# Cross-attention on one core: fp16 pairs in place of fp32r pairs, all sixteen heads in one pass

## Chip, core and metric

The kernel runs on one core of one Trainium2 chip. The metric is the device time of the whole program in microseconds. Its engines are TensorE (PE in the profile; its weight loads are PEld), VectorE (DVE), ScalarE (ACT), GpSimd (POOL) and SyncE (SP), which here only issues DMAs.

## What is computed

Sixteen batches; 512 query rows, 512 context rows and width 512 in each; 16 heads of 64.

```python
Q = (x @ Wq + bq); K = (ctx @ Wk + bk); V = (ctx @ Wv + bv)      # 512 x 1024, split into 16 heads
scores = einsum('bhqd,bhkd->bhqk', Q, K) / 8 * mask
attn = softmax(scores, axis=-1)
out = einsum('bhqk,bhkd->bhqd', attn, V).reshape(b, s, 1024) @ Wo + bo
x = x + out
return (x - mean(x)) * rsqrt(var(x) + 1e-5) * gamma + beta
```

All inputs and outputs are float32. To keep near float32 precision, the kernel writes each operand of a matmul as a pair, a rounded value (hi) and the difference that the rounding left (lo), and adds three products for each: hi·hi, hi·lo and lo·hi.

## The kernel before, in words

Work is done in tiles of 128 partitions by 512 columns. Two heads make a *pair* (128 wide). The sixteen heads are cut into two groups of eight (`GROUPS = 2`, four pairs in a group); the program goes through all sixteen batches with the weights of group 0, then again through all sixteen with the weights of group 1, so there are 32 *half-batches*. After group 0 the sum x + bo + part of the output is stored to a DRAM buffer `partial`, and group 1 reads it back, adds its part and does the layer norm.

In each half-batch TensorE does:

- 16 *fills* (`fill`, lines 340 to 342): Q0 to Q3 and K0 to K3 (one pair of heads each), V0 to V3 (128 rows of the context each) and O0 to O3 (128 rows of the output each). Each is 4 contraction tiles times 3 products, 12 matmuls of 128x128 weights and 512 columns. The operands are fp32r.
- 16 *score queries* (`scores`, lines 388 to 394): for a pair and 128 query rows, two heads side by side in the two row halves of the array, 3 products: 3 steps of two matmuls each, fp32r.
- 4 *values* (`values`, line 423): for one pair, 12 steps of two matmuls in the two column halves of the array. The operands (probabilities and V) are already fp16 pairs.
- one 1-column matmul (L404), `bound_inputs`, for a bound on V from which its fp16 scale is made.

For each tile of 128x512 scores: DVE multiplies by the mask and takes the row maximum (`mask_and_max`, L709), POOL negates two maxima (`negate_max`, L976), ACT takes the exponential with its row sum (`exponentials`, L526), POOL scales four sums (L983), DVE inverts them (L718), ACT rounds the normalized tile to fp16 (`round_probs`, L539), DVE takes the fp16 difference (`split_probs`, L725), for one tile in eight POOL does instead, in two instructions (L991, L996). Then a DMA transpose on SP's queue brings the two heads' pieces of 128 query rows into `pT`. `score_ps` has four banks, so at most two score queries stand in PSUM; `probs` has eight tiles, so rounding may trail the exponentials by at most eight tiles.

A fill's result leaves PSUM in two instructions: ACT writes the hi part (L515 for Q and K, L507 for V, L549 for the context `ctx_ps`), DVE the lo part (L784, L789, L734). O leaves with one DVE instruction (L799). The inputs x and context (transposed on the host) come in as raw tiles: for x POOL rounds and subtracts (L965, L968); for the context ACT rounds (L496), DVE takes the maximum (L744), POOL subtracts (L968).

The order of the work on each engine is written out by hand in a `body` for each engine, each with the arguments `prev, here, nxt`; the bodies run as a software pipeline over the batches, with semaphores between engines. The three fill banks are shared out by the table `FILL_BANK`.

## Time and profile before

| | before |
|---|---|
| median of 3 runs | 2381.5 us (2380.4 to 2382.26) |
| the profiled execution | 2381.32 us, its span 2379.5 us |
| PE busy | 2299.0 us, 97% |
| DVE busy | 1983.5 us, 83% |
| ACT busy | 1789.5 us, 75% |
| POOL busy | 1263.9 us, 53% |
| DMA | 446 MB, queues 78% busy |
| granted TensorE clock | 0.989 |

The span runs from the first to the last instruction. Busy times are from the start of an instruction to its end, and instructions of one engine overlap (a matmul takes 390 ns from start to end, but the next begins 229 ns after it began). So the pace of an engine is read from the starts of instructions that follow each other without a wait, not from their durations.

### The profile page before, as it was taken

Reading aid. Unit: us, or ns where it says so; the run is one execution under the profiler, and the core shown is the slowest. Engines: PE = TensorE matmul, PEld = TensorE weight load, DVE = VectorE, ACT = ScalarE, POOL = GpSimd, SP = SyncE. Lnnn points to the kernel's source line nnn. Section 1 sums busy time; section 2 is a strip of 40 time slices with the busy share of each in tenths; the row PEclk is TensorE's granted clock in tenths of the full one; section 3 lists DMA queues with packets and bytes.
Section 4 is the critical chain, followed back from the end, with each engine's and each line's share of the span. In section 5 each row is a group of like instructions: output and inputs, shape, how many; then the busy total and the mean of one; then the engine's idle time right before and its main releaser. Section 6 shows DMA issues by size and latency. Waiting matters only on the chain.

```text
span 2379.5 us, 47987 instructions
## 1 busy us (share of the span) xinstructions
PE 2299.0 (97%) x12352; PEld 1565.4 (66%) x12352; DVE 1983.5 (83%) x4296; ACT 1789.5 (75%) x3809; POOL 1263.9 (53%) x1704
## 2 busy tenths in 40 slices
PE   5899999999999999999899999999999999999994
PEld 4566666666666666666566666666666666666662
DVE  5788888888788888788787989988989988999883
ACT  4777777777777777777677877788887778777773
POOL 2454444555444555444443666565666665666645
PEclk9999999999999999999999999999999999999997
DMA  3978878777878787877879888778778777777764
GB/s 129 195 174 195 203 184 191 189 194 185 206 188 191 183 198 181 206 190 190 200 183 203 189 190 198 192 187 198 191 187 192 195 188 196 188 189 193 197 158 115
DMA packets 1165324, 446.02 MB, mean 187 GB/s; under 512 B 1078880, under 2 KB 1078880, under 8 KB 1165280
## 3 DMA queue, kind: packets, MB, share of 16 engines
q1 hardware_dynamic: 1161728, 444.70, 77.6%
q10 hardware_dynamic: 3552, 0.80, 0.2%
q8 instruction: 19, 0.31, 0.1%
q14 instruction: 25, 0.20, 0.0%
HBM read 143.41 MB, written 33.55 MB: 74 GB/s over the span
## 4 chain that ended last, share of the span: by engine, by line
PE 93%; DVE 2%; DMA 2%; POOL 1%; ACT 1%; issue 1%; SPq 0%; POOLq 0%; DVEq 0%
PE fill_ps L340 22%; PE fill_ps L341 19%; PE fill_ps L342 19%; PE ctx_ps L423 14%; PE score_ps L388 8%; PE score_ps L391 5%; PE score_ps L394 5%; DMA pT<-p 1%; DVE score_ps L709 1%; DMA raw<-in_ct 0%; DVE p L725 0%; SPq L232 0%; POOL acc L1039 0%; POOL acc L1041 0%; ACT probs L526 0%
## 5 line engine op out<-in xcount | busy, mean ns | idle before, releaser
L709 DVE CUSTOM_DVE_ANT_0 score_ps<-score_ps,mask_sb 128x512 f32<-128x512 f32 x1024 | 693.4, 705 | 279.8 <-PE score_ps L394 272.0
L526 ACT ACTIVATE probs<-score_ps,neg_max 128x512 f32<-128x512 f32 x1024 | 696.6, 684 | 300.1 <-POOL neg_max L976 297.8
L725 DVE SCALAR_TENSOR_TENSOR p<-probs,inv_sum,p 128x512 f16<-128x512 f32 x896 | 750.9, 857 | 49.6 <-ACT p L539 49.6
L539 ACT ACTIVATE p<-probs,inv_sum 128x512 f16<-128x512 f32 x1024 | 706.6, 718 | 29.9 <-DVE inv_sum L718 24.9
L976 POOL TENSOR_SCALAR neg_max<-row_max 128x2 f32<-128x2 f32 x512 | 173.2, 338 | 628.2 <-DVE row_max L709 622.0
L423 PE MATMUL ctx_ps<-pT,v 128*64 128x512 f16 x3072 | 364.9, 388 | 16.4 <-DMA pT<-p 8.5
L423 PEld LDWEIGHTS ctx_ps<-pT,v 128*64 128x64 f16 x3072 | 168.3, 111 | 198.4 <-issue 72.5
L388 PE MATMUL score_ps<-k_hi,q_hi 64*128 64x512 f32 x1024 | 250.9, 477 | 17.0 <-ACT probs L526 15.3
L340 PE MATMUL fill_ps<-xT_hi,wq_hi 128*128 128x512 f32 x512 | 216.1, 422 | 24.1 <-DVE wq_lo L699 24.0
L340 PE MATMUL fill_ps<-cT_hi,wk_hi 128*128 128x512 f32 x512 | 210.7, 412 | 3.4 <-POOL cT_lo L968 2.2
L340 PE MATMUL fill_ps<-wo_hi,ctx_hi 128*128 128x512 f32 x512 | 211.9, 414 | 0.8 <-DVE acc L799 0.8
L340 PE MATMUL fill_ps<-wv_hi,cT_hi 128*128 128x512 f32 x512 | 207.2, 405 | 1.5 <-DVE k_lo L784 1.5
L388 PEld LDWEIGHTS score_ps<-k_hi,q_hi 64*128 64x128 f32 x1024 | 97.7, 183 | 168.1 <-issue 132.9
L391 PE MATMUL score_ps<-k_hi,q_lo 64*128 64x512 f32 x1024 | 207.0, 394 | 0.0
L394 PE MATMUL score_ps<-k_lo,q_hi 64*128 64x512 f32 x1024 | 205.5, 392 | 0.0
L526 ACT ACTIVATION_READ_ACCUMULATOR probs<-score_ps,neg_max 128x1 f32 x1024 | 203.0, 198 | 0.0
L341 PE MATMUL fill_ps<-xT_hi,wq_lo 128*128 128x512 f32 x512 | 202.0, 394 | 0.0
L341 PE MATMUL fill_ps<-wo_hi,ctx_lo 128*128 128x512 f32 x512 | 201.9, 394 | 0.0
L342 PE MATMUL fill_ps<-wo_lo,ctx_hi 128*128 128x512 f32 x512 | 201.9, 394 | 0.0
L342 PE MATMUL fill_ps<-xT_lo,wq_hi 128*128 128x512 f32 x512 | 201.0, 393 | 0.0
L342 PE MATMUL fill_ps<-wv_lo,cT_hi 128*128 128x512 f32 x512 | 200.5, 392 | 0.0
L341 PE MATMUL fill_ps<-cT_hi,wk_lo 128*128 128x512 f32 x512 | 200.4, 391 | 0.0
(71 smaller groups left out, 4226.6 us busy)
## 6 DMA issues: line engine op xcount, KB each, us to landing
raw<-in_xt SPq DMA_DIRECT2D x128, 256.0 KB, 3.1
raw<-in_ct SPq DMA_DIRECT2D x128, 256.0 KB, 3.3
mask_sb<-in_mask_Bx1xSxS_fk SPq DMA_DIRECT2D x128, 256.0 KB, 2.9
acc<-in_x SPq DMA_DIRECT2D x64, 256.0 KB, 2.9
partial<-acc SPq DMA_DIRECT2D x64, 256.0 KB, 2.4
acc<-partial SPq DMA_DIRECT2D x64, 256.0 KB, 2.8
out<-acc SPq DMA_DIRECT2D x64, 256.0 KB, 2.1
pT<-p SPq DMA_TRANSPOSE x512, 3.8
```

The source lines that it names most:

```text
L340: nc.tensor.matmul(bank, lhs[0], rhs[0], start=is_first, stop=False)
L341: nc.tensor.matmul(bank, lhs[1], rhs[0], start=False, stop=False)
L342: return nc.tensor.matmul(bank, lhs[0], rhs[1], start=False, stop=is_last)
L388: nc.tensor.matmul(banks[a], qk_hi["q"][halves[a], par, cols], qk_hi["k"][halves[a], par, :], start=True, stop=False)
L391: nc.tensor.matmul(banks[a], qk_lo["q"][halves[a], par, cols], qk_hi["k"][halves[a], par, :], start=False, stop=False)
L394: nc.tensor.matmul(banks[a], qk_hi["q"][halves[a], par, cols], qk_lo["k"][halves[a], par, :], start=False, stop=True).then_inc(s_ready, 1)
L423: mm = nc.tensor.matmul(ctx_ps[a * DH:(a + 1) * DH, :], v_piece[piece][:, t, col:col + DH], pT[:, par, :, a, plane, t, :], start=is_first, ...
L526: nc.scalar.activation(probs[:, i % E_TILES, :], score_ps[:, i % 4, :], ACT.Exp, bias=neg_max[:, p % 2, i:i + 1], accum_out=row_sum[:, p % ...
L539: nc.scalar.activation(p16[:, q, a, 0, :], probs[:, i % E_TILES, :], ACT.Copy, scale=inv_sum[:, p % 2, i:i + 1]).then_inc(p_rounded, 1)
L709: nc.vector.tensor_tensor_reduce(out=score_ps[:, i % 4, :], in0=score_ps[:, i % 4, :], in1=mask_sb[:, q, :], scale=SCORE_SCALE, scalar=-3. ...
L725: nc.vector.scalar_tensor_tensor(out=p16[:, q, a, 1, :], in0=probs[:, i % E_TILES, :], scalar=inv_sum[:, p % 2, i:i + 1], in1=p16[:, q, a, ...
L976: nc.gpsimd.tensor_scalar(neg_max[:, p % 2, cols], row_max[:, p % 2, cols], -1.0, 1.0, ALU.mult, ALU.mult).then_inc(max_negated, 1)
```

## The change

All operands become pairs of fp16 values, and all sixteen heads are done in one pass over the batches; the weights of all heads stay in SBUF. In detail:

- `GROUPS` is gone; a batch has eight pairs. It has 28 fills: Q0 to Q7, K0 to K7, V0 to V7 (12 matmuls each) and O0 to O3, which now go over eight contraction tiles (24 matmuls each). 32 score queries and 8 values as before. The `partial` buffer, its stores and loads are gone, as is every second load and rounding of x, the context and the mask.
- As fp16 has a short exponent, x, the context and each weight are scaled. `weight_maxima`, `weight_scale`, `weight_bound` on DVE with `sum_weight_rows` on PE make a scale for each weight once, at the start, and all tiles of a weight wait for it. For each batch, `input_maximum` (now x too), `bound_products`, `bound_inputs`, `input_scale` make the scales of x, the context and V from bounds.
- Splitting an input tile: ACT rounds both x and the context, with the scale; POOL scales the raw tile in place (`tensor_scalar`) and subtracts (`tensor_tensor`, fp16 out).
- bv is folded into the output bias: once, at the start, eight float32 matmuls `bias_output` and one DVE addition. `values` of the first pair waits for it.
- Weights are loaded into staging areas that lie over `probs`, `p16`, `pT` and `ctx16`; the first use of each of these waits for the weight's split.
- The hand-written orders of all engines are new.

```diff
-GROUPS = 2
-GH = H // GROUPS
-GW = GH * DH
-PAIRS = GH // 2
+WIDTH = H * DH
+PAIRS = H // 2
+GROUP = 4
+GW = GROUP * P
...
-        w_hi = {w: sb(f"w{w}_hi", [P, 4, GW], F32R) for w in "qkvo"}
-        xc_hi = {t: sb(f"{t}T_hi", [P, DT, S], F32R) for t in "xc"}
-        qk_hi = {t: sb(f"{t}_hi", [P, 2, S], F32R) for t in "qk"}
-        qk_lo = {t: sb(f"{t}_lo", [P, 2, S], F32R) for t in "qk"}
-        v_piece = [sb(f"v{i}", [P, KT, GW], F16) for i in range(2)]
+        w16 = {w: sb(f"w{w}16", [P, DT, 2, WIDTH], F16) for w in "qkv"}
+        w16["o"] = sb("wo16", [P, PAIRS, 2, D], F16)
+        xc16 = {t: sb(f"{t}T16", [P, DT, 2, S], F16) for t in "xc"}
+        qk16 = {t: sb(f"{t}16", [P, 2, 2, S], F16) for t in "qk"}
+        v16 = sb("v16", [P, 1, KT, 2, GW], F16)
...
+            def start():
+                load_input(0, "x", range(DT), early=True)
+                load_weight("q")
+                load_input(0, "c", range(DT), early=True)
+                load_weight("k")
+                load_mask(0, range(QT), early=True)
+                load_weight("v")
...
+            def bias_output():
+                pe.wait_ge(vo_back_ready, 1)
+                pe.wait_ge(scale_ready, 3)
+                pe.wait_ge(bias_in, 3 * DMA)
+                for j in range(PAIRS):
+                    mm = nc.tensor.matmul(ctx_ps[:, :], bias_col["v"][:, j:j + 1].to_broadcast([P, P]), staged["o"][:, j, :],
+                                          start=j == 0, stop=j == PAIRS - 1)
+                mm.then_inc(bias_out_ready, 1)
...
+                parts = PAIRS if kind == "O" else DT
+                for j in range(parts):
...
+                        lhs, rhs = [w16[w][:, j, l, cut] for l in (0, 1)], [xc16[t][:, j, l, :] for l in (0, 1)]
...
+            def input_scale(n):
+                if is_first(n):
+                    return
+                dve.wait_ge(bias_scaled, 2 * n)
+                dve.wait_ge(undo_ready, n)
+                dve.wait_ge(score_scale_ready, n)
+                dve.wait_ge(v_scale_ready, n)
+                for t in "xc":
+                    dve.wait_ge(xc_split[t], n * DT)
+                take_bound(slice(0, 3), bound_no(n))
...
+                    wait_alone(pool, xc_rounded[t], n * DT + i + 1)
+                    wait_alone(pool, xc_max_taken[t], n * DT + i + 1)
+                    nc.gpsimd.tensor_scalar(raw_input(t, i), raw_input(t, i), scale[:, c:c + 1], 1.0, ALU.mult,
+                                            ALU.mult).then_inc(xc_scaled[t], 1)
+                    wait_alone(pool, xc_scaled[t], n * DT + i + 1)
+                    nc.gpsimd.tensor_tensor(xc16[t][:, i, 1, :], raw_input(t, i), xc16[t][:, i, 0, :],
+                                            ALU.subtract).then_inc(xc_split[t], 1)
```

The order of TensorE in one batch after the change, as its `body` has it (Q3 is a fill, s2 one score query of pair 2, v0 the values of pair 0, b the bound; a name with ' belongs to the next batch, O0 with the last fills of the row to the same batch and O1 to O3 to the one before):

```
Q3 O1 V3 s2 s2 O2 K3 v0 s3 s3 O3 s3 K4 Q4 s3 K5 s4 Q5 s4 v1 s4 Q6 s4 v2 s5 K6 s5 b' Q7 s5 v3 s5 V4 s6 K7
s6 V5 s6 V6 s6 V7 s7 s7 v4 Q0' s7 K0' s7 v5 Q1' s0' K1' s0' v6 s0' Q2' s0' V0' s1' K2' s1' v7 s1' O0 s1' s2' V1' V2' s2'
```

## Rows read from the trace of the kernel before

**Rows 1.** The page: the chain that ended last, shares of the span by engine.

```profile
PE 93%; DVE 2%; DMA 2%; POOL 1%; ACT 1%; issue 1%; SPq 0%; POOLq 0%; DVEq 0%
```

**Rows 2.** The bound's matmul L404 in two windows: durations, first and last start, count.

```profile
L404 PEld LDWEIGHTS ctx_ps<-small,bound_part x26: 187/188/188, 193.9 to 1047.9; 128*128 128x128 f32 x26
...
L404 PEld LDWEIGHTS ctx_ps<-small,bound_part x28: 187/188/188, 1351.6 to 2276.8; 128*128 128x128 f32 x28
```

**Rows 3.** Timeline of PE: start us, duration us, then line and operation; a score query, then a fill.

```profile
1502.12 0.39 PE L394 MATMUL score_ps<-k_lo,q_hi 64*128 64x512 f32 x2
1502.45 0.50 PE L340 MATMUL fill_ps<-xT_hi,wq_hi 128*128 128x512 f32 x1
1502.79 0.39 PE L341 MATMUL fill_ps<-xT_hi,wq_lo 128*128 128x512 f32 x1
...
1505.08 0.39 PE L342 MATMUL fill_ps<-xT_lo,wq_hi 128*128 128x512 f32 x1
```

**Rows 4.** Timeline of PE: the end of a V fill, and the values (all 24, then the first 4).

```profile
1498.52 0.39 PE L342 MATMUL fill_ps<-wv_lo,cT_hi 128*128 128x512 f32 x1
1498.84 2.78 PE L423 MATMUL ctx_ps<-pT,v 128*64 128x512 f16 x24
...
1498.84 0.62 PE L423 MATMUL ctx_ps<-pT,v 128*64 128x512 f16 x4
```

**Rows 5.** Groups by line with their forms: weight loads in fp32r and fp16, then POOL's.

```profile
L423 PEld LDWEIGHTS ctx_ps<-pT,v 128*64 128x64 f16 x3072 | 168.3, 111 | 198.4 <-issue 72.5
L391 PEld LDWEIGHTS score_ps<-k_hi,q_lo 64*128 64x128 f32 x1024 | 98.3, 186 | 4.1
...
L996 POOL TENSOR_TENSOR p<-probs,p 128x512 f16<-128x512 f32 x128 | 168.6, 1317 | 21.9 <-POOL probs L991 20.5
```

**Rows 6.** Windows: length, busy us of PE, PEld, DVE, ACT, POOL, then clock.

```profile
1517.40:1535.40 18.00, 18.00 (x99) 12.21 (x98) 17.36 (x37) 13.38 (x30) 13.22 (x18) 1.00 0.74 171
1463.40:1534.60 71.20, 71.20 (x389) 48.64 (x387) 64.05 (x138) 56.55 (x121) 44.22 (x58) 1.00 0.79 192
803.80:875.00 71.20, 71.20 (x389) 48.64 (x387) 58.31 (x130) 54.12 (x117) 34.82 (x50) 1.00 0.79 192
```

**Rows 7.** Timeline of ACT in a stretch where one instruction follows the other.

```profile
1476.66 0.68 ACT L526 ACTIVATE probs<-score_ps,neg_max 128x512 f32<-128x512 f32 x1
...
1477.33 0.69 ACT L549 ACTIVATE ctx_hi<-ctx_ps,small 128x512 fp32r<-128x512 f32 x1
1477.90 1.33 ACT L539 ACTIVATE p<-probs,inv_sum 128x512 f16<-128x512 f32 x2
```

**Rows 8.** Timeline of DVE in such a stretch: mask, K's difference, mask, two of the probabilities'.

```profile
1491.41 0.68 DVE L709 CUSTOM_DVE_ANT_0 score_ps<-score_ps,mask_sb 128x512 f32<-128x512 f32 x1
...
1492.02 0.73 DVE L784 SCALAR_TENSOR_TENSOR k_lo<-fill_ps,bk_col,k_hi 128x512 fp32r<-128x512 f32 x1
1492.68 1.40 DVE L725 SCALAR_TENSOR_TENSOR p<-probs,inv_sum,p 128x512 f16<-128x512 f32 x2
```

**Rows 9.** Two DVE lines, window 1230 to 2300: ns min/median/max; and L725's mean of the whole.

```profile
L725 DVE SCALAR_TENSOR_TENSOR p<-probs,inv_sum,p x420: 710/745/1778, 1230.6 to 2297.7; 128x512 f16<-128x512 f32 x140
...
L784 DVE SCALAR_TENSOR_TENSOR q_lo<-fill_ps,bq_col,q_hi x60: 739/744/752, 1256.8 to 2293.7; 128x512 fp32r<-128x512 f32 x60
...
L725 DVE SCALAR_TENSOR_TENSOR p<-probs,inv_sum,p 128x512 f16<-128x512 f32 x896 | 750.9, 857 | 49.6 <-ACT p L539 49.6
```

**Rows 10.** Timeline of the start: first x tile, first scores, last quarter of V's weights.

```profile
16.14 0.63 POOL L965 TENSOR_SCALAR xT_hi<-raw 128x512 fp32r<-128x512 f32 x1 [15.21 <-DMA raw<-in_xt]
...
35.84 0.50 PE L388 MATMUL score_ps<-k_hi,q_hi 64*128 64x512 f32 x2 [1.66 <-DVE k_lo L784]
...
40.95 0.69 DVE L699 TENSOR_TENSOR wv_lo<-raw,wv_hi 128x512 fp32r<-128x512 f32 x1
```

**Rows 11.** Timeline of the end: PE's last long wait and its last rows shown.

```profile
2344.85 4.94 PE L423 MATMUL ctx_ps<-pT,v 128*64 128x512 f16 x24 [8.49 <-DMA pT<-p]
...
2361.17 0.40 PE L342 MATMUL fill_ps<-wo_lo,ctx_hi 128*128 128x512 f32 x1
```

1754 lines of the change are left out of this document (1028 added, 726 removed).

## The prediction

> **What bounds the kernel now.** First the page's chain and busy times: PE is 93% of the chain that ended last [rows 1] and busy 97% of the span; every other engine has idle time. A busy PE may still be a waiting one, so next the period of the work. The bound's matmul fires once in each half-batch: 26 times from 193.9 to 1047.9 us in pairs of two instructions (13 half-batches, 12 periods) gives 854.0 / 12 = 71.17 us, and in the second group 925.2 / 13 = 71.17 us [rows 2]. I use 71.15. Group 1 has the layer norm on top (DVE 64.05 us busy of 71.2 against 58.31, POOL 44.22 against 34.82) and still the same period with PE full [rows 6]. So in steady state PE alone sets the time, down to its pace per matmul, and DVE at 90% beside it costs nothing. 32 periods are 2276.8 us; the other 102.7 us of the span are the start, the end and the change of groups. Of these the change of groups has about 19: between the windows of [rows 2] lie 1351.6 - 1047.9 = 303.7 us for four periods, 284.6.
>
> **PE's period, taken apart.** In a fill one fp32r matmul follows the other every 0.229 us ((1505.08 - 1502.79) / 10) [rows 3]. A score step in fp32r takes about 0.23. In the values, fp16 already, the last of 12 steps starts 2.78 - 0.38 = 2.40 us after the first, and the second 0.62 - 0.38 = 0.24 after it, which leaves 2.16 / 10 = 0.216 a step [rows 4]. Each change of the array's form (whole array, row halves, column halves) costs more: from the last score step to the fill 0.33 instead of 0.23, and then 0.34 instead of 0.229 for the fill's second matmul, together 0.21 [rows 3]; into the values 0.32 and 0.24, together 0.115 over the pace [rows 4]. The second part goes with the weight load that nothing hides: it is 0.11 behind a 128-column fp32r load and 0.024 behind two 64-column fp16 loads. Sum for a half-batch: 192 fill matmuls x 0.229 = 44.0; 48 score steps x 0.23 = 11.0; 48 value steps x 0.216 = 10.4; 30 changes of form, 26 at 0.2 and 4 at 0.115 = 5.7; in all 71.1 us. The measured 71.15 is all explained, without any wait.
>
> **Part 1: fp16 on TensorE.** A batch after the change has 28 fills, of which four are double: 384 matmuls, 96 score steps, 96 value steps, as many as two half-batches. At the fp16 pace that the values show it is 576 x 0.216 = 124.4 us. The order in the text has 60 changes of form, again as many as in two half-batches. Eight go into values (0.115 each, 0.9 us). For the other 52 the trace shows no fp16 load of 128 columns; the nearest rows are 64 columns in fp16, 111 ns, and 128 in fp32r, 186 ns [rows 5]. That gives bounds of 0.115 and 0.20 for each change; I take 0.15, as the exposed part should grow with the columns and halve with the bytes: 7.8 us (6.0 to 10.4). Sum 133.1 us for a batch against 142.3 now: 9.2 us less, 147 in sixteen batches. Here the Trainium skill, in "TensorE: Matmul & The Clock Gate", section LDWEIGHTS, speaks against me: it says that a load's time goes by its columns alone. By that rule the change of form would stay at the upper bound and the batch would take 135.8. The same page of the Trainium skill, in its section on Fast Weight Load, says that non-fp32 loads of 128 columns can run about twice as fast. No row here shows either for 128 columns in fp16.
>
> **Part 2: what goes and comes on the others.** By [rows 6], two half-batches (one of each group) cost DVE 122.4 us busy, ACT 110.7, POOL 79.0. A batch after drops four O evacuations on DVE (3.0), takes 4 maxima of x and 4 of the context instead of 8 of the context (0), one bound more (0.2): 119.6, 0.90 of 133.1, the same share as group 1 has now. ACT rounds four x and four context tiles for eight context tiles (0): 110.7, 0.83. POOL subtracts eight tiles instead of sixteen, at 1.32 each in the form with fp16 out [rows 5], and scales these eight instead of rounding eight: about 11 us less, 68 of 133. Stores and loads of `partial` and half of the input traffic go: nothing waited for them, so zero; if that cover (PE's full period) were gone, a 256 KB load would be 3 us in landing.
>
> **Part 3: a dense stretch.** The new order isn't even. From the last score query of pair 3 to that of pair 7 it has 16 queries with 12 fills and 4 values between: on PE 240 steps x 0.216 + 32 changes x 0.145 = 56.4 us for half of the scores, and the other half has 76.7 us. On ACT, by the starts in [rows 7]: 32 exponentials x 0.67 (with the read of the sum) = 21.4, 31 roundings x 0.61 = 18.9, 18 evacuations x 0.57 = 10.3, 8 roundings of inputs at about 0.55 = 4.4, 3 normalizations x 0.7 = 2.1: 57.1 us. On DVE by [rows 8] and [rows 9]: 32 masks x 0.62 = 19.8, 28 differences x 0.77 = 21.6 (0.66 from start to start, and 0.11 of delay, the mean of 857 less the median of 745), 18 x 0.66 = 11.9 for the lo parts, inverses, a maximum, bounds and register work about 3: 56.3. All three are full, and four score banks and eight `probs` tiles are all the slack, some 3.5 us. Now the densest stretch seen is 18 us with DVE at 17.36 and PE still full [rows 6]; for 56 us nothing in this trace shows it. What PE loses here it can't win back in the other half, where it is the bound itself. I take 2.9 us a batch, about 5% of the stretch; from below 0, from above the second rival. Batch: 136.0.
>
> **Part 4: start and end.** 102.7 less 19 leaves 83.7 for both. The end: PE waits 8.49 us for the last transposes, takes 4.94 instead of 2.78 for the values behind them, and 18 us follow its last matmul (2361.2 to 2379.5) [rows 11]; that is 29, and with shorter waits ahead of it I set the end at 40, an estimate. The start is the rest, 43.7. The end stays at 40: the same chain of work, with O fills of twice the length that are counted above. The start grows. Now a fill waits for one quarter of a weight at a time, and the first scores start at 35.8 [rows 10]. After, the whole of Wq must be loaded (3 MB with x before it; the first x tile waited until 16.1 for 3 MB of weights [rows 10]), its maxima taken, summed through PE, scaled and split: scale of x at 24. `scale_biases` stands ahead of x's fourth tile on POOL and needs K's scale too, for which Wk goes the same way: 39. POOL's context tiles then take 2.1 each: K0 at 51, the first scores at 56, 20 later. Then DVE takes maxima and splits of all of Wv in one go (4 x 1.2 + 8 x 0.7 + 2 = 12, now four quarters of some 1.3 each beside other work, the last of them split at 41 [rows 10]): 7 more. The same for Wo, with PE waiting, 9, and eight float32 matmuls at some 0.6 to 0.9 each, 5. Together 41 more: 85 (65 to 100). The change of groups, 19, falls away.
>
> **Sum.** 16 x 136.0 + 85 + 40 - 3 (the first batch has no previous work) = 2298 us of span; the profiled execution is 1.8 us over its span now and near the median (2381.32 and 2381.5), so 2300 us, 3.4% less.
>
> **The rivals.**
> - *The stretch costs nothing* (the order hides it as group 1 does now): 16 x 133.1 + 122 + 2 = 2254 us. For it: DVE at 17.36 of 18 us without a wait on PE. Against: its length and ACT full at the same time.
> - *Weight loads stay as exposed as in fp32r*: 135.8 + 2.9 a batch, 2343 us. For it: each fp16 load seen has half the columns. This is what the column rule of the Trainium skill, cited in part 1, comes to.
> - *The change doesn't do what it says on PE*: fp16 fills keep 0.229 a step as well. 384 x 0.229 + 96 x 0.23 + 96 x 0.216 + 11.3 = 142.0 a batch, the stretch then has room: 2396 us, slower. Against it: values step at 0.216 in the same array.
> - *DVE becomes the bound in the stretch* (the other side). A difference of probabilities takes 0.745 as a rule, but 1.78 at worst, while the same operation on PSUM never goes over 0.752 [rows 9]: the one that reads two SBUF tiles waits out a GpSimd instruction. In the stretch GpSimd does all its splits of inputs, and 28 such differences run. If half are hit, 14 x 1.03 = 14.4 in place of the 3.1 counted: 11 us more a batch, 144.1, 2430 us. It decides from (2381.5 - 124) / 16 = 141.1 on, 8 over the floor, that is 11 of 28 hit. The Trainium skill's "SBUF — State Buffer", in its part on the shared port pair, has this as a lock that is held for the whole instruction; with that rule the trace agrees (1.78 against 0.745). Against the rival: DVE's mean loss is 0.11 now with POOL at 53% busy, and POOL has less to do after.
>
> **How the numbers follow.** Forecast 0.50 (2270 to 2330), no cost of the stretch 0.18, exposed loads 0.12, fp16 no faster 0.06, DVE bound 0.14. A difference under 0.2% (about 5 us) can't be told from none in a measurement of this kernel. The first three are faster, 0.80, and of the last 0.03 that end short of 141 a batch: 0.83 faster. 0.03 lie around the break-even point, and 0.14 are slower. The range leaves out the cases over 2372 and the best part of the first rival: 2236 to 2372.
>
> **What would show it.** Per batch, by the bound's matmul: 136 us. Steps of 0.216 in fills and 0.15 for a change of form; if these are right and the period isn't, the loss must stand as PE waits on ACT's exponentials or a lo part, between the scores of pairs 4 and 7. First scores near 56 us. DVE near 0.88 of the period. The prediction is wrong if fp16 fills don't step at 0.216, if PE waits over 8 us in each batch, or if the start is far from 85.

## The result, and the profile after

| | before | after |
|---|---|---|
| median | 2380.95 us (2378.5 to 2382.3, 4 runs) | 2346.07 us (2344.5 to 2348.2, 4 runs) |
| span of the profiled execution | 2379.5 us | 2344.9 us |
| period of a batch | 142.3 us | 138.2 us |
| granted TensorE clock | 0.989 | 0.968 |

The ratio is 0.9855 [0.9838, 0.9872], 1.45% less time; I had predicted 2300 us, 3.4% less, with a range of 2236 to 2372. The time lies in the range, but 46 us over the forecast.

The page of the kernel after: busy time, the granted clock in 40 slices of the span, and the chain that ended last by engine (before: [rows 1]).

```profile
PE 2185.3 (93%) x12348; PEld 883.0 (38%) x12348; DVE 2020.0 (86%) x4283; ACT 1788.3 (76%) x3809; POOL 1055.4 (45%) x1576
...
PEclk9799999999999999999999999999999999999997
...
PE 78%; ACT 9%; DVE 5%; issue 4%; POOL 2%; SPq 1%; DMA 1%; ACTq 0%; DVEq 0%; POOLq 0%
```

PE had 93% of the chain and has 78%: the rest of the chain now runs over the other engines. The period, as in [rows 2], from the bound's matmul, which is L401 now and fires once in a batch:

```profile
L401 PE MATMUL ctx_ps<-small,ones x30: 242/252/272, 171.0 to 2105.8; 128*128 128x3 f32 x30
```

15 firings of two instructions, 14 periods: 1934.8 / 14 = 138.2 us, where I had said 136.0. What stays for start and end is 2344.9 - 16 x 138.2 = 133.7 us, where I had said 122. So of the missing 46 us, about 35 are in the period (16 x 2.2) and 12 at the edges.

**TensorE's own pace.** The timeline of PE after, a V fill, a score query and a V fill (compare [rows 3]); then weight loads by line and form, busy us and mean ns (compare [rows 5]).

```profile
1154.43 0.38 PE L407 MATMUL fill_ps<-wv,cT 128*128 128x512 f16 x1
1154.74 0.82 PE L458 MATMUL score_ps<-k,q 64*128 64x512 f16 x6
1155.50 0.39 PE L405 MATMUL fill_ps<-wv,cT 128*128 128x512 f16 x1
1155.72 0.38 PE L406 MATMUL fill_ps<-wv,cT 128*128 128x512 f16 x1
...
1157.88 0.38 PE L407 MATMUL fill_ps<-wv,cT 128*128 128x512 f16 x1
```

```profile
L479 PEld LDWEIGHTS ctx_ps<-pT,v 128*64 128x64 f16 x3072 | 177.4, 117 | 247.8 <-issue 106.9 <-DVE v L1024 27.4
L458 PEld LDWEIGHTS score_ps<-k,q 64*128 64x128 f16 x3072 | 121.9, 94 | 320.8 <-issue 128.0 <-ACT probs L640 126.5
...
L406 PEld LDWEIGHTS fill_ps<-wv,cT 128*128 128x128 f16 x512 | 50.3, 98 | 49.4 <-issue 0.6
```

A fill steps at (1157.88 - 1155.72) / 10 = 0.216 us, and the second matmul after a change of form comes after 0.22, where in fp32r it was 0.34. To see how much of a period is TensorE's own pace and how much is loss, I added up the distances between the starts of matmuls that follow each other, from 446 to 2100 us (12 batches): 1574.7 us at the paces just shown, 23.8 us over them in steps of twice the length, 55.3 us of waits. Scaled to a batch that is **131.6 + 2.0 + 4.6 us**. My floor was 133.1.

**Where the loss stands.** Nearly all of it stands at one place of each batch, from the first scores of pair 7 through the values of pair 4. The timeline of PE there (in brackets the idle time before the row and what ended it):

```profile
1161.64 0.39 PE L458 MATMUL score_ps<-k,q 64*128 64x512 f16 x1
1163.21 0.82 PE L458 MATMUL score_ps<-k,q 64*128 64x512 f16 x5 [1.18 <-ACT probs L640]
1164.48 0.39 PE L458 MATMUL score_ps<-k,q 64*128 64x512 f16 x1 [0.46 <-ACT probs L640]
1165.16 0.86 PE L458 MATMUL score_ps<-k,q 64*128 64x512 f16 x5 [0.28 <-ACT probs L640]
1167.43 5.33 PE L479 MATMUL ctx_ps<-pT,v 128*64 128x512 f16 x24 [1.41 <-DVE v L1024]
1172.69 0.39 PE L405 MATMUL fill_ps<-xT,wq 128*128 128x512 f16 x1
```

The values take 5.33 us instead of the 2.78 of [rows 4] (in every second batch; in the others 4.2 to 4.5, and so periods of 137.7 and 138.8 us take turns). Four windows (length, then busy us of PE, PEld, DVE, ACT, POOL, then the clock): the stretch that part 3 of the prediction summed up, from the last scores of pair 3 to the last of pair 7; a whole period; the nine microseconds around the values; and the time in which GpSimd works on the next batch's input tiles.

```profile
1115.70:1178.84 63.14, 59.28 (x340) 23.11 (x340) 56.63 (x130) 56.28 (x121) 39.22 (x56) 0.95 0.75 145
1153.00:1291.10 138.10, 134.25 (x769) 54.12 (x768) 123.03 (x263) 109.78 (x236) 65.43 (x99) 0.98 0.79 160
1166.50:1175.50 9.00, 8.07 (x38) 3.19 (x40) 5.46 (x10) 6.88 (x14) 8.23 (x10) 0.66 0.58 118
...
1151.60:1176.40 24.80, 21.05 (x106) 7.72 (x105) 19.72 (x40) 20.70 (x45) 22.61 (x29) 0.86 0.65 126
```

Around the values the clock is granted at 0.66, between its two levels, 1.2 and 2.4 GHz: the lower one for most of the nine microseconds. In the last window GpSimd, 45% busy over the span, is busy for 22.61 of 24.80 us and never idle for over 0.2 us at a time.

Followed back, from GpSimd, ScalarE and VectorE in the same microseconds:

```profile
1157.22 0.69 POOL L1305 TENSOR_SCALAR raw<-raw,small 128x512 f32<-128x512 f32 x1
1158.09 1.43 POOL L1308 TENSOR_TENSOR xT<-raw,xT 128x512 f16<-128x512 f32 x1 [0.18 <-POOL raw L1305]
...
1160.21 0.19 POOL L1325 TENSOR_SCALAR neg_max<-row_max 128x2 f32<-128x2 f32 x1
...
1160.52 0.69 ACT L640 ACTIVATE probs<-score_ps,neg_max 128x512 f32<-128x512 f32 x1 [1.83 <-POOL neg_max L1325]
...
1163.04 0.72 ACT L608 ACTIVATE cT<-raw,small 128x512 f16<-128x512 f32 x1
...
1165.59 0.70 ACT L619 ACTIVATE v<-fill_ps,small 128x512 f16<-128x512 f32 x1
...
1157.76 2.31 DVE L1003 SCALAR_TENSOR_TENSOR p<-probs,inv_sum,p 128x512 f16<-128x512 f32 x2
...
1166.63 0.74 DVE L1024 SCALAR_TENSOR_TENSOR v<-fill_ps,small,v 128x512 f16<-128x512 f32 x1
```

The negation of maxima that is due at about 1158 stands on GpSimd behind the next batch's x tiles and comes at 1160.21; ScalarE is idle for 1.83 us until then. From there everything is late: the exponentials, which release the score banks (PE's waits at 1163 and 1164), and V7's high part at 1165.59, behind them and two context tiles, then V7's low part at 1166.63, for which the values wait. (That V7 is late because the negation was is a reading of these rows alone, and the run with short tiles below speaks against it.) Two differences of VectorE take 2.31 us beside GpSimd's subtraction, where two took 1.40 in [rows 8].

**The edges.** The timeline of PE at the start (compare [rows 10]):

```profile
13.72 0.56 PE L379 MATMUL ctx_ps<-small,ones 128*128 128x4 f32 x2 [13.72 <-DVE small L873]
...
28.33 0.59 PE L379 MATMUL ctx_ps<-small,ones 128*128 128x4 f32 x2 [11.85 <-DVE small L873]
...
60.91 0.59 PE L379 MATMUL ctx_ps<-small,ones 128*128 128x4 f32 x2 [5.47 <-DVE small L873]
...
67.86 1.46 PE L458 MATMUL score_ps<-k,q 64*128 64x512 f16 x5 [3.92 <-ACT probs L640]
...
107.97 0.60 PE L379 MATMUL ctx_ps<-small,ones 128*128 128x8 f32 x2 [9.39 <-DVE small L873]
109.47 9.62 PE L392 MATMUL ctx_ps<-wo_staged,bv_col 128*128 128x512 f32 x16 [0.89 <-DVE small L1285]
```

PE waits for the maxima of Wq, Wk, Wv and Wo (L873), one after the other, 9.39 us for the last, and the float32 matmuls of `bias_output` take 9.62 us. From 0 to 171 us PE is idle for 66 us, and loses some 15 more in steps of twice the length. At the end it waits 6.36 and 7.07 us for the transposes of the last two pairs, where [rows 11] has one such wait of 8.49.

### The profile page after: what moved, and what is told of

Its sections match the earlier page's. It is cut to its first block, busy times and chain, and to the rows that moved or that the text cites. A ratio compares the mean times of both kernels' runs of the same rounds, so it can differ in the third digit from the quotient of the medians.

```text
span 2344.9 us, 46357 instructions
## 1 busy us (share of the span) xinstructions
PE 2185.3 (93%) x12348; PEld 883.0 (38%) x12348; DVE 2020.0 (86%) x4283; ACT 1788.3 (76%) x3809; POOL 1055.4 (45%) x1576
## 4 chain that ended last, share of the span: by engine, by line
PE 78%; ACT 9%; DVE 5%; issue 4%; POOL 2%; SPq 1%; DMA 1%; ACTq 0%; DVEq 0%; POOLq 0%
PE fill_ps L405 17%; PE fill_ps L406 16%; PE fill_ps L407 16%; PE ctx_ps L479 15%; PE score_ps L458 13%; ACT probs L640 4%; ACT p L654 3%; DVE score_ps L989 2%; ACT xT L608 1%; ACT v L619 1%; DVE p L1003 1%; DVE v L1024 1%; POOL neg_max L1325 0%; DVE small L873 0%; PE ctx_ps L392 0%
## 5 line engine op out<-in xcount | busy, mean ns | idle before, releaser
L640 ACT ACTIVATE probs<-score_ps,neg_max 128x512 f32<-128x512 f32 x1024 | 699.6, 686 | 297.5 <-POOL neg_max L1325 261.9
L989 DVE CUSTOM_DVE_ANT_0 score_ps<-score_ps,mask_sb,small 128x512 f32<-128x512 f32 x1024 | 753.2, 753 | 171.4 <-PE score_ps L458 166.6
L1003 DVE SCALAR_TENSOR_TENSOR p<-probs,inv_sum,p 128x512 f16<-128x512 f32 x896 | 774.2, 881 | 9.0 <-ACT p L654 7.0
L1325 POOL TENSOR_SCALAR neg_max<-row_max 128x2 f32<-128x2 f32 x512 | 185.4, 362 | 856.3 <-DVE row_max L989 853.0
L458 PE MATMUL score_ps<-k,q 64*128 64x512 f16 x3072 | 434.2, 381 | 41.7 <-ACT probs L640 41.7
L479 PE MATMUL ctx_ps<-pT,v 128*64 128x512 f16 x3072 | 393.1, 410 | 41.0 <-DVE v L1024 26.1
L458 PEld LDWEIGHTS score_ps<-k,q 64*128 64x128 f16 x3072 | 121.9, 94 | 320.8 <-issue 128.0
L405 PE MATMUL fill_ps<-wv,cT 128*128 128x512 f16 x512 | 195.8, 382 | 6.0 <-DVE q L1018 6.0
L405 PE MATMUL fill_ps<-xT,wq 128*128 128x512 f16 x512 | 197.5, 386 | 3.5 <-POOL xT L1308 3.5
L405 PE MATMUL fill_ps<-cT,wk 128*128 128x512 f16 x512 | 196.6, 384 | 1.8 <-POOL cT L1308 1.8
L406 PE MATMUL fill_ps<-xT,wq 128*128 128x512 f16 x512 | 196.3, 383 | 0.0
L407 PE MATMUL fill_ps<-xT,wq 128*128 128x512 f16 x512 | 196.2, 383 | 0.0
L406 PE MATMUL fill_ps<-cT,wk 128*128 128x512 f16 x512 | 195.6, 382 | 0.0
L405 PE MATMUL fill_ps<-wo,ctx 128*128 128x512 f16 x512 | 194.7, 380 | 0.8 <-DVE acc L1032 0.8
L407 PE MATMUL fill_ps<-cT,wk 128*128 128x512 f16 x512 | 195.4, 382 | 0.0
L406 PE MATMUL fill_ps<-wv,cT 128*128 128x512 f16 x512 | 194.6, 380 | 0.0
L407 PE MATMUL fill_ps<-wv,cT 128*128 128x512 f16 x512 | 194.6, 380 | 0.0
L406 PE MATMUL fill_ps<-wo,ctx 128*128 128x512 f16 x512 | 194.0, 379 | 0.0
L407 PE MATMUL fill_ps<-wo,ctx 128*128 128x512 f16 x512 | 194.0, 379 | 0.0
```

The costliest lines, as they stand in the source:

```text
L405: nc.tensor.matmul(bank, lhs[0], rhs[0], start=is_start, stop=False)
L406: nc.tensor.matmul(bank, lhs[1], rhs[0], start=False, stop=False)
L407: return nc.tensor.matmul(bank, lhs[0], rhs[1], start=False, stop=is_last)
L458: mm = nc.tensor.matmul(banks[a], qk16["q"][halves[a], par, lq, cut], qk16["k"][halves[a], par, lk, :], start=lq == lk, stop=lk == 1)
L479: mm = nc.tensor.matmul(ctx_ps[a * DH:(a + 1) * DH, :], v16[:, g % 1, t, piece, col:col + DH], pT[:, par, :, a, plane, t, :], start=t == 0 ...
L640: nc.scalar.activation(probs[:, i % E_TILES, :], score_ps[:, i % 4, :], ACT.Exp, bias=neg_max[:, p % 2, i:i + 1], accum_out=row_sum[:, p % ...
```

## The experiments

Each was compared with the kernel before on the same chip; the times are medians, with the ratio to before. "Period" is that of L401. Each expectation names its own theories A and B; they aren't the same ones from run to run.

**Orders moved by hand, one place at a time.** First, the fill Q0' goes ahead of the values that wait for V7:

```diff
-                    values(here, 4)
                 if nxt is not None:
                     fill(nxt, "Q", 0)
                 if here is not None:
+                    values(here, 4)
                     scores(here, 7, range(2, 3))
```

> One swap in TensorE's order: the fill Q0 of the next batch goes ahead of the values of pair 4; nothing is left out. In the changed kernel a batch takes 138.25 us: about 131.6 at PE's own pace, 4.6 of waits, and 2.0 of slow steps (12 value steps at 0.425 in place of 0.216 right behind a wait of 1.5 us on V7's lo part). Theory A (a local pile-up: three engines come late at one place, scores 7(0) to values 4, and the granted clock falls behind it): the fill covers the wait on V7, so 1.5 us of wait and most of the slow steps go, 134.5 to 136 us a batch, 2290 to 2320 us in all. Theory B (DVE and ACT are full over the whole dense stretch, and set its length): a wait taken away here comes back at the next scores; 137.5 to 138.3 a batch, 2335 to 2348 us.

2346.98 us, 0.9859 [0.9843, 0.9875]: the same as after. The wait for V7 is gone, and so is half of the loss by the clock, but PE, earlier by that, waits at K0' for the context's tiles from GpSimd:

```profile
896.50 0.39 PE L405 MATMUL fill_ps<-cT,wk 128*128 128x512 f16 x1 [0.74 <-POOL cT L1308]
...
899.10 0.39 PE L405 MATMUL fill_ps<-cT,wk 128*128 128x512 f16 x1 [1.78 <-POOL cT L1308]
```

Next, V7's halves on ScalarE and VectorE ahead of the context's tiles and of masks:

```diff
                     exponentials(here, 6, range(5, 6))
+                    evacuate(here, "V", 7)
+                    exponentials(here, 6, range(6, 8))
...
                     invert_sums(here, 6, 0)
-                    mask_and_max(here, 7, range(0, 2))
-                    split_context(here, 3)
-                    mask_and_max(here, 7, range(2, 3))
                     evacuate(here, "V", 7)
+                    mask_and_max(here, 7, range(0, 3))
```

> Nothing left out; on ACT the hi part of V7 goes ahead of two exponentials and of the roundings of the context's first two tiles, on DVE the lo parts of V7 and of the context of pair 3 go ahead of the masks of pair 7. The values of pair 4 then find V7 some 1.5 us earlier. Theory D (after the swap of Q0, whose wait came back at the fill K0 on POOL's differences of the context's tiles: the input chain ACT round, POOL scale, POOL subtract ends only when K0 needs it): the wait moves to K0 and the period stays 137.5 to 138.5 us, 2335 to 2350 in all. Theory A (one local wait and the clock behind it): 134.5 to 136 a batch, 2290 to 2320.

2350.41 us, 0.9873 [0.9857, 0.989], period 139.2. Again the wait for V7 goes and K0' waits, 1.2 and 1.9 us. (The idle times before K0's matmuls are 1.05 and 1.78 us in most batches; 1.2 and 1.9 count from start to start.) These are two ways to take the visible wait away, and both uncover the same next one.

GpSimd's negations ahead of the second of two x tiles and of its own difference:

```diff
                 if nxt is not None:
-                    split_input(nxt, "x", range(1, 3))
+                    split_input(nxt, "x", range(1, 2))
                 if here is not None:
                     scale_sums(here, 6, 0)
                     negate_max(here, 6, range(2, 3))
-                    split_probs(here, 5, range(7, 8))
+                if nxt is not None:
+                    split_input(nxt, "x", range(2, 3))
+                if here is not None:
                     negate_max(here, 6, range(3, 4))
+                    split_probs(here, 5, range(7, 8))
```

> Nothing left out; only POOL's order: the negation of the maxima of tiles 4 and 5 of pair 6 goes ahead of x's third input tile, and that of tiles 6 and 7 ahead of POOL's share of the probabilities of pair 5. Theory E (order on POOL: these negations stand behind input tiles of 1.9 us, ACT idles 1.8 us for them and the scores 7(0) come 1.4 us late): the wait before scores 7(0) shrinks by half at least and the period falls by 1 to 2 us, 2315 to 2332 in all. If DVE's blocked differences alone make the masks late: no change at 7(0), 2342 to 2350.

2342.09 us, 0.9837 [0.982, 0.9853]. The wait in pair 7's first query falls from 1.18 to 0.73 us, but that of the second grows from 0.46 and 0.28 to 1.06: GpSimd's difference now holds the tile of `probs` that a later exponential needs. 4 us in all. VectorE's differences at this place no longer meet GpSimd's long instructions (from 14 to 30 us behind the bound's matmul their mean is 766 ns over the batches, against 968 in the kernel after), and that alone is worth no more than these 4 us.

This order, V7 early and the fourth x tile earlier on ScalarE, together:

```diff
                     round_probs(here, 5, range(6, 8))
+                if nxt is not None:
+                    round_input(nxt, "x", range(3, 4))
+                if here is not None:
                     exponentials(here, 6, range(4, 5))
                     evacuate(here, "V", 6)
-                if nxt is not None:
-                    round_input(nxt, "x", range(3, 4))
...
-                    split_probs(here, 5, range(4, 6))
+                    split_probs(here, 5, range(4, 5))
                     mask_and_max(here, 6, range(6, 8))
+                    split_probs(here, 5, range(5, 6))
                     evacuate(here, "V", 5)
+                    split_context(here, 3)
```

> As the run before, and on ACT the exponentials of tiles 5 to 7 of pair 6 go ahead of the roundings of the context's first tile (which wait for the last fill V7 on PE), x's last tile ahead of tile 4, and V7's hi part ahead of both context tiles; on DVE two masks go ahead of a difference, and the lo parts of V7 and of the context of pair 3 earlier. Theory E in full (orders on three queues, not throughput, make the pile-up): all three waits shrink to under 1 us together, the clock stays high, and K0 waits 2 to 4 us for the context's tiles instead: 135.5 to 137 a batch, 2300 to 2325. Theory B (no slack in the stretch): 138 or more, 2345 and more.

And with K0' behind the last scores of pair 7, and the earlier weight maxima that are told below:

```diff
-                if nxt is not None:
-                    fill(nxt, "K", 0)
                 if here is not None:
                     scores(here, 7, range(3, 4))
                     values(here, 5)
+                if nxt is not None:
+                    fill(nxt, "K", 0)
```

> As the run before, with the reordered start of e8_start (12 us in its own run), and K0 of the next batch on PE, ACT and DVE behind the last scores of pair 7 and the values of pair 5, so that the context's four tiles have 3.5 us more. If theory E and the input chain (D) are the whole cause: 133 to 135 a batch, 2245 to 2285 in all. If something in the new order comes late in its turn (scores 0(0) behind K0, or values 5 behind its transposes): 135 to 138, 2290 to 2330.

2357.69 us, 0.99 [0.9883, 0.9916], and 2408.39 us, 1.0118 [1.0101, 1.0135]: slower, the second one slower than before the change. In the first, ScalarE waits for a VectorE difference of the tile eight back, which frees its place in `probs` (timeline of ACT); in the second, with K0' moved, PE waits longest right behind that place (timeline of PE).

```profile
1169.52 0.69 ACT L640 ACTIVATE probs<-score_ps,neg_max 128x512 f32<-128x512 f32 x1 [1.82 <-DVE p L999]
```

```profile
1195.20 0.55 PE L458 MATMUL score_ps<-k,q 64*128 64x512 f16 x1 [2.05 <-ACT probs L640]
1196.93 1.46 PE L458 MATMUL score_ps<-k,q 64*128 64x512 f16 x5 [1.19 <-ACT probs L640]
```

**Work taken away, one engine at a time.** In each of these the output is incomplete in all batches but the first: the columns left out stand where an earlier batch left them. First GpSimd scales and subtracts 64 of 512 columns of the input tiles:

```diff
+                    w = S if is_first(n) else 64
-                    nc.gpsimd.tensor_scalar(raw_input(t, i), raw_input(t, i), scale[:, c:c + 1], 1.0, ALU.mult,
+                    nc.gpsimd.tensor_scalar(raw_input(t, i)[:, :w], raw_input(t, i)[:, :w], scale[:, c:c + 1], 1.0, ALU.mult,
```

> POOL scales and subtracts only 64 of 512 columns of each input tile from the second batch on (the lo parts of the other columns are left from the first batch). This takes some 12 us of POOL work from the dense stretch and nothing from DVE or ACT. Theory C (DVE's differences of probabilities wait out POOL's instructions, and this delays masks and exponentials at the pile-up): the mean of these differences falls from 881 to about 850 ns or less, none beside an input tile takes 1.5 us, and the waits before scores 7(0) and 7(1) shrink: 135 to 136.5 us a batch, 2300 to 2320 us. Theories A and B without C: 2335 to 2347.

2321.93 us, 0.9756 [0.974, 0.9772], period 136.6: 24 us less than after. The wait for V7 stays whole (timeline of PE; then by line VectorE's differences, which were at 881 in the kernel after):

```profile
1155.04 4.36 PE L479 MATMUL ctx_ps<-pT,v 128*64 128x512 f16 x24 [1.46 <-DVE v L1024]
```

```profile
L1003 DVE SCALAR_TENSOR_TENSOR p<-probs,inv_sum,p 128x512 f16<-128x512 f32 x896 | 740.3, 843 | 9.5 <-ACT p L654 7.1
```

In the dense stretch alone the mean of these differences falls more, from 882 to 799 ns, 2.3 us of VectorE's time in each batch. So this edit takes away two things at once, what stands ahead of the negations on GpSimd and what GpSimd's instructions cost VectorE.

Then ScalarE's rounding of the input tiles, 64 of 512 columns of those tiles:

```diff
+                    w = S if is_first(n) else 64
-                    nc.scalar.activation(xc16[t][:, i, 0, :], raw_input(t, i), ACT.Copy,
+                    nc.scalar.activation(xc16[t][:, i, 0, :w], raw_input(t, i)[:, :w], ACT.Copy,
```

> ACT rounds only 64 of 512 columns of each input tile from the second batch on, some 3 us of ACT's work a batch, all of it in the dense stretch; POOL and DVE keep theirs. Theory D (POOL's 1.9 us per tile set the input chain, not ACT's 0.6) and the theory of DVE waiting out POOL: little, 137 to 138 a batch, 2330 to 2345. Theory B, with ACT as the full engine: 3 us of the 6.6 go at once, 135 to 136 a batch, 2300 to 2320.

2338.94 us, 0.9824 [0.9808, 0.984]: 7 us less. And masks and exponentials of 384 columns for seven tiles in eight:

```diff
+                    w = S if is_first(n) and p == 0 or i in POOL_TILES else 384
-                    nc.scalar.activation(probs[:, i % E_TILES, :], score_ps[:, i % 4, :], ACT.Exp,
+                    nc.scalar.activation(probs[:, i % E_TILES, :w], score_ps[:, i % 4, :w], ACT.Exp,
```

> Masks and exponentials cover 384 of 512 columns, but for the first pair and POOL's tile. This takes 0.13 us from 56 masks and 0.11 us from 56 exponentials a batch: 7.5 us of DVE and 6 us of ACT, half of it in the dense stretch. Theory B (the two engines are full there): all waits ahead of scores 7(0), 7(1) and values 4 go, 132 to 134 a batch, 2245 to 2280 us. Theory D and POOL's part: the waits on the exponentials shrink by half, the one on V7 and the slow steps may stay, 135 to 137, 2295 to 2325.

2317.17 us, 0.9729 [0.9713, 0.9745], period 136.6: 29 us less, though 7/8 of all exponentials are 0.11 us shorter and of all masks 0.13 us, which frees VectorE of 119 us and ScalarE of 97 in the whole run (the masks' busy time 753.2 to 634.3, the exponentials' 699.6 to 602.9). The waits stay, smaller:

```profile
1148.64 0.82 PE L458 MATMUL score_ps<-k,q 64*128 64x512 f16 x5 [0.84 <-ACT probs L641]
1149.82 0.39 PE L458 MATMUL score_ps<-k,q 64*128 64x512 f16 x1 [0.35 <-ACT probs L641]
...
1152.63 4.47 PE L479 MATMUL ctx_ps<-pT,v 128*64 128x512 f16 x24 [1.33 <-DVE v L1026]
```

This is as much as GpSimd's short tiles gave, so it doesn't decide between the engines; the run with V7 early and GpSimd's tiles short, below, leaves both of these engines their full work.

**The mask's scale as a constant.** The mask instruction reads its scale from an SBUF column since the change. With a constant in its place (a stand-in value, so the scores are scaled otherwise):

```diff
-                        scale=score_scale, scalar=-3.0e38, op0=ALU.mult, op1=ALU.max,
+                        scale=SCORE_SCALE * 1.0e-4, scalar=-3.0e38, op0=ALU.mult, op1=ALU.max,
```

> The mask instruction takes its scale as a constant again and not from an SBUF column; the scale's value is a stand-in, so the scores are scaled otherwise. In the changed kernel this instruction takes 753 ns in the mean, 705 in the kernel before. If the column costs the difference, it returns to about 705 (and from start to start from 0.66 to 0.61), 3 us less DVE work a batch. Theory B (DVE full in the dense stretch, 32 masks there): 1.5 us at least of the 6.6 us of waits and slow steps go, 2300 to 2325 us. Theory A: the masks come 0.1 us earlier at the pile-up, 0 to 1 us a batch, 2330 to 2346. If it is not the column, 753 ns stays, and so does the time.

2335.84 us, 0.9812 [0.9795, 0.9828], 10 us less. By line, of the kernel after and then of this one:

```profile
L989 DVE CUSTOM_DVE_ANT_0 score_ps<-score_ps,mask_sb,small 128x512 f32<-128x512 f32 x1024 | 753.2, 753 | 171.4 <-PE score_ps L458 166.6
```

```profile
L989 DVE CUSTOM_DVE_ANT_0 score_ps<-score_ps,mask_sb 128x512 f32<-128x512 f32 x1024 | 699.0, 699 | 197.0 <-PE score_ps L458 195.4
```

The column costs 54 ns in each of 1024 masks. Two more runs tried to have this back with nothing left out, by moving the scale into GpSimd's negation and ScalarE's exponential, the second with the start of the next experiment:

```diff
-                                         bias=neg_max[:, p % 2, i:i + 1],
+                                         bias=neg_max[:, p % 2, i:i + 1], scale=score_scale,
...
-                        scale=score_scale, scalar=-3.0e38, op0=ALU.mult, op1=ALU.max,
+                        scale=1.0, scalar=-3.0e38, op0=ALU.mult, op1=ALU.max,
```

> The score scale leaves VectorE's mask instruction (whose scale becomes the constant 1.0) and goes where a column is read anyway: GpSimd multiplies the two maxima by it where it multiplied by -1, ScalarE's exponential takes it as its scale. The output stays what it was. VectorE waits for the last exponential of the batch before the next scale is written. Theory A (the column costs VectorE 53 ns in each mask, and nothing in the other two): masks of 0.70 instead of 0.753 us, 2336 us (2332 to 2340), as with the constant scale. Theory B (the column costs on ScalarE what it costs on VectorE): exponentials of 0.74 instead of 0.686, no gain or a loss, 2346 to 2365 us.

> The scale moved into the exponential and the earlier weight maxima at the start, together; the output stays what it was. The two gains lie in different parts of the span, so they should add: first bound matmul at 158, period 137.6; 2346 - 10 - 12 = 2324 us (2318 to 2330). If the scale moved costs on ScalarE, 2334 or above.

2387.11 us, 1.0031 [1.0021, 1.004], and 2371.94 us, 0.9969 [0.9957, 0.9981]: 41 and 26 us slower than after. By line, exponential and negation, of the kernel after and then of the first of these:

```profile
L640 ACT ACTIVATE probs<-score_ps,neg_max 128x512 f32<-128x512 f32 x1024 | 699.6, 686 | 297.5 <-POOL neg_max L1325 261.9 <-DVE p L1003 31.0
...
L1325 POOL TENSOR_SCALAR neg_max<-row_max 128x2 f32<-128x2 f32 x512 | 185.4, 362 | 856.3 <-DVE row_max L989 853.0
```

```profile
L640 ACT ACTIVATE probs<-score_ps,neg_max,small 128x512 f32<-128x512 f32 x1024 | 793.2, 778 | 262.5 <-POOL neg_max L1325 232.2 <-DVE p L1003 25.0
...
L1325 POOL TENSOR_SCALAR neg_max<-row_max,small 128x2 f32<-128x2 f32 x512 | 231.8, 453 | 819.1 <-DVE row_max L989 785.5 <-ACT probs L640 27.6
```

A column more costs ScalarE 92 ns in each exponential and GpSimd 91 in each negation, and VectorE's wait for the last exponential of a batch was added. The Trainium skill, "ScalarE: Activation LUTs", section "What ACT_TABLE_LOAD costs", states about 93 ns for each such operand of an activation; with that the trace agrees (686 to 778). I had expected none. In the whole run 54 us are freed on VectorE, 94 are spent on ScalarE and 46 on GpSimd, and the sum is a loss of 41 us, with the period at 141; how the loss divides among the exponentials, the negations and the added wait isn't shown.

**The clock.** Eight matmuls whose results nobody reads, in the time in which PE waits ahead of the values of pair 4:

```diff
+            def busy_work(count):
+                pe.wait_ge(*users[0])
+                for i in range(count):
+                    nc.tensor.matmul(fill_ps[:, 0, :], w16["k"][:, 0, 0, 0:P], w16["k"][:, 0, 1, 0:GW], start=True, stop=True)
...
                     scores(here, 7, range(0, 2))
+                    busy_work(8)
                     values(here, 4)
```

> Eight matmuls of no use (1.7 us, into the fill bank that Q0 will start afresh) stand ahead of the values of pair 4, where PE waits 1.5 us for V7. Nothing is left out. If the slow steps behind come from the granted clock falling because PE stood idle in this place, they go: 2.0 us a batch less, minus up to 0.5 by which the added work outlasts the wait: 2315 to 2330 us. If the clock falls anyway (for the waits before, or for a reason outside), the time stays or grows: 2345 to 2370.

2335.9 us (2330.7 to 2347.6), 0.9806 [0.9788, 0.9825]. The loss in steps of twice the length falls from 24 to 11 us, and in steady state the values of pair 4 take 2.78 us again in nearly all batches. So the clock's fall comes from the idle time there, and it is worth some 10 us. Together with the start and GpSimd's order:

> The three edits that took time off while leaving the computation whole, in one kernel: the earlier weight maxima at the start (12 us less by itself), GpSimd's negations ahead of the third x tile (4 us less by itself), and eight unused matmuls ahead of the fifth values, in the time in which TensorE waits there (10 us less by itself). Theory A (each loss is of its own: the start is outside the loop, the wait for the exponentials and the clock behind it are two things): the gains add, 2346 - 12 - 4 - 10 = 2320 us (2314 to 2328), first bound matmul at 158, period 137.2. Theory B (one chain of waits: what is taken off in one place comes back in the next, and the unused matmuls stand in the way once the wait ahead of them is shorter): only the start's gain stays whole, 2328 to 2336 us, the period stays at 137.7 or above.

2337.9 us (2330.7 to 2345.1), 0.9811 [0.9779, 0.9843]: the gains don't add. These two kernels scatter by 17 and 14 us, where most others do by 1 to 5 (the two with the scale moved by 9 and 14). In their traces two or three periods are 5 to 8 us longer than the rest, by a single wait for nothing that the profile shows (timeline of PE):

```profile
653.97 0.61 PE L405 MATMUL fill_ps<-xT,wq 128*128 128x512 f16 x1 [4.25 <-issue]
```

The kernel after has none; what it waits for stays open.

**The start.** The maxima of Wv and Wo are taken earlier on VectorE, while it waits, and `sum_weight_rows` and `bias_output` move up on PE:

```diff
                     nc.vector.tensor_scalar(qk_back, w_total["q"][:, 1:2], w_total["k"][:, 1:2], SCORE_SCALE, ALU.mult,
                                             ALU.mult).then_inc(qk_back_ready, 1)
+                    weight_maxima("v")
...
                     evacuate(nxt, "Q", 0)
+                if opening:
+                    weight_maxima("o")
```

> Nothing left out; only the start is reordered. DVE takes the maxima of Wv and Wo where it idles for the first fills (36 to 48 us), PE sums them behind K0, Wo's scale follows Wv's, and the eight float32 matmuls of the output bias (9.6 us) run while DVE splits Wv. In the changed kernel PE waits 6 and 4.5 us around 55 to 68 us, 9.8 us for Wo's maxima at 98 and computes 9.6 us of bias behind it. If these waits are what makes the start long, the time falls by 15 to 25 us, to 2321 to 2331, with the period at 138.25. If other waits take their place (DVE still splits both weights in 5.4 us each ahead of masks), less than 8 us.

2334.21 us, 0.9807 [0.9791, 0.9823]: 12 us less, all of it ahead of the first L401 (157.9 instead of 171.0 us); the period stays. I had expected 15 to 25 if PE's waits were what makes the start long. The eight float32 matmuls still take 8.83 us, now ahead of the scores, and the first values wait 4.09 us for V's low part.

**GpSimd's tiles and V7's place, together.** By now the rival theories were that GpSimd's input tiles are the next limit at this place, or that ScalarE and VectorE have no room there whoever releases them. GpSimd's tiles cut to 64 columns and V7 early, together:

> Two edits in one: GpSimd scales and subtracts only 64 of 512 columns of the input tiles (their low parts are then wrong for the rest, in all batches but the first), and the orders of ScalarE and VectorE put V7's two halves earlier, which by itself moved the wait from the fifth values to K0', where TensorE then waited 1.2 + 1.9 us for the context's tiles from GpSimd. Theory A (GpSimd's chain of input tiles is the next in line, at K0'): with it short the wait for V7 is gone and doesn't return, the period goes from 136.6 (GpSimd short alone) to 134 to 135, 2282 to 2300 us. Theory B (ScalarE and VectorE have no room in this stretch, whoever releases them): the wait comes back before scores or K0' on an exponential or a difference, and the period stays at 136 or above, 2314 us or more.

2279.24 us, 0.9574 [0.9558, 0.959]. Alone the first edit gave 24 us and the second took 4; together they give 67. The bound's matmul, a window over one batch, and what is left of the waits:

```profile
L401 PE MATMUL ctx_ps<-small,ones x28: 242/248/252, 305.7 to 2047.8; 128*128 128x3 f32 x28
```

```profile
1119.60:1254.00 134.40, 132.62 (x775) 54.07 (x776) 122.06 (x264) 110.58 (x238) 56.52 (x99) 1.00 0.82 165
```

```profile
1135.80 0.39 PE L458 MATMUL score_ps<-k,q 64*128 64x512 f16 x1 [0.95 <-ACT probs L640]
1136.47 0.82 PE L458 MATMUL score_ps<-k,q 64*128 64x512 f16 x5 [0.28 <-ACT probs L640]
```

(2047.8 - 305.7) / 13 = 134.0 us, the clock at 1.00 for the whole batch, no wait at V7 or K0', 2.4 us of waits a batch. VectorE and ScalarE work as much as ever (122.06 and 110.58 us of 134.4, against 123.03 and 109.78 of 138.1). This is the decisive run, and it shows two limits, one behind the other. The wait for V7 comes from where V7's halves stand on ScalarE and VectorE: with GpSimd's tiles short alone it stayed at 1.46 us. The wait at K0' behind it comes from GpSimd's tiles: with V7 early alone it appeared, and with short tiles it is gone. ScalarE and VectorE have room for both. What isn't shown is how much of the gain is GpSimd's order and how much is VectorE no longer blocked by it (the mean in the stretch is 799 ns here too), nor what V7 early gives beside shorter masks and exponentials with GpSimd whole. All reliefs together, with the eight matmuls:

> All the reliefs together: GpSimd's and ScalarE's work on input tiles cut to 64 of 512 columns, masks and exponentials of seven tiles in eight cut to 384 columns (so the output is wrong in all of these), the mask's scale a constant, and eight unused matmuls ahead of the fifth values. TensorE's real work is unchanged. Theory A (all of the lost time in a batch is waits behind the three other engines and the clock's fall after these; TensorE's own pace is 131.6 us): period 132.5 to 134 us, the unused matmuls among it (1.7), 2255 to 2285 us. Theory B (something of TensorE's own, or of the transposes, costs part of it): the period stays above 135.

2294.5 us (2274.1 to 2305.7), 0.9665 [0.9646, 0.9684]. The period is 133.85 us in all but the odd batch with a gap like the one above (139.7), 1.7 of it the unused matmuls: 132.1 for the rest, half a microsecond over TensorE's own 131.6. So waits on the other three engines, and the clock behind them, are all that holds TensorE back.

**With the computation whole.** GpSimd's tiles can't be left out, but they can stand elsewhere: in the run with V7 early it is idle for 3.63 and 2.47 us among the negations of pair 5.

```diff
-                    negate_max(here, 5, range(0, 3))
+                    negate_max(here, 5, range(0, 1))
+                if prev is not None:
+                    scale_and_shift(prev, range(1, 2))
+                if here is not None:
+                    negate_max(here, 5, range(1, 2))
+                if nxt is not None:
+                    split_input(nxt, "x", range(0, 1))
```

The other two x tiles follow one negation earlier each; V7 early and the new start are in it too.

> Nothing is left out here, only orders are changed: V7's halves earlier on ScalarE and VectorE (alone no gain, the wait moved to K0'), the earlier weight maxima at the start (12 us less alone), and on GpSimd the work that stands ahead of the dense place moved into its idle time among the maxima of pair 5: one row block's scale and shift (2.9 us) up by three negations, the first two input tiles (1.9 us each) up by two or three. Theory A (GpSimd's work on input tiles, at the place where it stands, is what holds ScalarE's exponentials and K0'): the waits before the scores of pair 7 and at K0' shrink as with GpSimd's tiles cut short, period 134 to 135.5 us, 2262 to 2290 us. Theory B (with GpSimd's work whole the wait only moves again, as with every order so far): period 137 or more, 2315 to 2335 us.

2314.41 us (2313.8 to 2315.5), 0.9718 [0.9697, 0.974], period 137.4 (137.0 in most batches). The wait for V7 is gone, and most of the clock's fall (about 5 us of 24 are left), but K0' still waits as in the second experiment (timeline of PE):

```profile
1152.92 0.39 PE L405 MATMUL fill_ps<-cT,wk 128*128 128x512 f16 x1 [1.05 <-POOL cT L1307]
...
1155.52 0.39 PE L405 MATMUL fill_ps<-cT,wk 128*128 128x512 f16 x1 [1.78 <-POOL cT L1307]
```

Last, the fourth context tile's difference as one VectorE instruction, and the fourth x tile earlier:

```diff
+            def split_last_context(n):
+                wait_alone(dve, xc_rounded["c"], (n + 1) * DT)
+                wait_alone(dve, xc_split["c"], n * DT + DT - 1)
+                nc.vector.scalar_tensor_tensor(
+                    out=xc16["c"][:, DT - 1, 1, :], in0=raw_input("c", DT - 1), scalar=scale[:, 1:2],
+                    in1=xc16["c"][:, DT - 1, 0, :], op0=ALU.mult, op1=ALU.subtract).then_inc(xc_split["c"], 1)
```

> Nothing is left out. On top of the last kernel (e20), whose period is 137.4 us with 1.2 + 1.9 us of wait at K0' for the context's last two tiles from GpSimd: the fourth x tile is rounded and split ahead of exponential 6(2), in GpSimd's idle 3.5 us; the fourth context tile's difference goes from two GpSimd instructions (about 2 us) to one of VectorE (about 0.7), into VectorE's idle 2.0 us; one negation goes ahead of the third context tile. Theory A (GpSimd's chain of tiles is what K0' waits for, 3.1 us a batch): nearly all of it goes, period 134.3 to 135.5, 2265 to 2285 us. Theory B (the next wait in line takes its place: exponential 6(2) and what follows is later by the rounding ahead of it, VectorE by its wait for the third tile): period 136.5 or more, 2300 to 2320 us.

2307.43 us (2305.9 to 2308.8), 0.9689 [0.9673, 0.9705], period 136.6. K0' waits 1.6 us a batch (idle time, as in the rows above) instead of 2.8 and the clock no longer falls, but waits of 0.3 to 0.5 us appear elsewhere. It is the fastest whole version here, 3.1% under the kernel before and 1.6% under the one after. By order alone, and one difference moved to VectorE, 1.6 of the 4.2 us a batch that the decisive run gains are had with nothing left out.

## Why the prediction was right or wrong, by its steps

- *What bounds the kernel before*: right. TensorE's pace fell by the predicted amount and the time followed in part.
- *Part 1, fp16 on TensorE*: right, and a little better than said. Steps of 0.216 us as predicted. The floor is 131.6 us; less the 124.4 of steps and about half a microsecond for the bound, that leaves 6.7 us for 60 changes of form, 0.11 each, where I took 0.15 (0.115 to 0.20). A 128-column fp16 load takes 98 ns, not more than the 111 of 64 columns. The Trainium skill's rule in "TensorE: Matmul & The Clock Gate", section LDWEIGHTS, that columns alone set a load's time, is not what the trace shows: 128 columns take 186 ns in fp32r [rows 5] and 98 in fp16. The same page of the Trainium skill says of Fast Weight Load that weights of 128 columns that aren't fp32 load about twice as fast; with that the trace agrees (98 against 186).
- *Part 2, the other engines' work*: near. DVE 123.0 us a batch for 119.6: 64 masks with 54 ns more each are 3.5 us, a cost that I didn't see, as I took the mask instruction for unchanged. ACT 109.8 for 110.7, POOL 65.4 for 68.
- *Part 3, the dense stretch*: here the prediction failed, in size and in mechanism. The stretch takes 62.6 us (62.0 and 63.1 in turn), where I had 56.4 + 2.9. The work was summed up well: about 56 us for PE without its losses, DVE at 56.63 (56.3 said) and ACT at 56.28 (57.1 said). The loss, too, stands where the prediction said to look for it, as waits on ScalarE's exponentials and on a low part. But it is 6.6 us a batch, 4.6 of waits and 2.0 by the clock, and the term of the sum that was mis-sized is the 2.9, taken as 5% of the stretch for PE, ACT and DVE being full together. They aren't what holds it: with DVE and ACT at their full work, V7 early and GpSimd's tiles short, the stretch takes 58.1 us. The step left out GpSimd, which has no line in its sum: over the stretch it is busy for 62%, but for 25 us towards its end it has no gap over 0.2 us; the negations stand there behind two input tiles of 1.9 us or more, and K0' gets its tiles from it. It left out the place of V7's halves in the orders of ScalarE and VectorE, and it had no term for the clock, which falls behind PE's waits.
- *Part 4, start and end*: 133.7 us for 122. The first scores started at 51.2, where I had 56, but PE waits 9.39 us for Wo's maxima and then has 9.62 of float32 matmuls, for which I had 9 and 5, and there are 5.47 us for Wv's and 3.92 behind them; the step that failed is the sum of what follows the first scores. How the 12 us divide between start and end was not worked out; 12 can be had back at the start by order alone.
- *The rivals*: none is what happened. "DVE becomes the bound" named GpSimd's lock on VectorE's differences. Their mean is 881 ns now, in the stretch 882, and 857 before [rows 9], so that is 28 x 0.025, under 1 us a stretch, not 11. That VectorE waits for GpSimd is seen, as 2.31 us for two differences. By the Trainium skill, "SBUF — State Buffer", section "Who interferes with whom", the loser is blocked for the whole instruction; a row with 2.31 for 1.4 fits it. With the tiles cut short the mean in the stretch falls to 799, so all of it that GpSimd's tiles cause is 28 x 0.083 = 2.3 us of VectorE's time; that isn't the 11 of the rival, but no run separates what it adds to the waits from what the order adds.
- *The sum*: floor 1.5 us a batch lower than said, loss 3.7 higher, so two misses partly cancel, which is luck; together 2.2 x 16 = 35 us, and 12 at the edges: the 47 us between the span of 2298 that I summed up and the 2344.9 measured.

## What to carry to other kernels

An engine at 45% busy can set the pace, as it may be full in just the place where the others need it (here 25 us of each 138). So sum up each engine over the dense place and not over the period, and name, for each negation, sum or scale of a few columns that others wait for, what is queued ahead of it on its own engine. A wait that moves when an order is changed may have a second limit behind it (here K0' behind V7): take both causes away together (V7 early was +4 us alone, and 43 us less on top of the short tiles) before giving up on either. A short wait of TensorE may cost more than its length, since its clock can fall behind it.

## What the runs showed of the hardware

- A scale from an SBUF column instead of a constant: 54 ns on VectorE's mask instruction (753 against 699), 92 ns on ScalarE's exponential (778 against 686), 91 ns on GpSimd's negation (453 against 362).
- A change of the array's form costs 0.11 us with fp16 operands (what is left of the floor of 131.6 us, over 60 changes), up to 0.21 with fp32r [rows 3].
- Behind waits of 1.18, 0.46, 0.28 and 1.41 us within six microseconds the granted clock fell to its lower level (0.66 in the mean of 9 us), and 24 matmuls took 5.33 us instead of 2.78. With waits of 0.95 and 0.28, in the kernel with V7 early and short tiles, it stayed at 1.00, and with eight unused matmuls in place of the 1.41 the 24 took 2.78.
- Float32 matmuls of 512 columns, of which the profile shows two rows each: 16 rows in 9.62 us. Those that start from 109.5 to 114.4 us, at a granted clock of 0.50, step at about 0.85 us, those behind 114.6, at 1.00, at 0.43.
- Two differences of probabilities on VectorE beside a GpSimd subtraction: 2.31 us instead of 1.40.
